# Queries and keys of a small attention layer in three TensorE blocks, and new orders on four engines, in a vision-transformer kernel

## The reference: what is computed

```python
def reference(x, ...):
    h = _L0_tok_ref(x, ...)                                   # 8 x 64 tokens x 192
    h = h + _L0_attn_ref(_layernorm(h, axis=-1), ...)
    h = h + _L0_ffn_ref(_layernorm(h, axis=-1), ...)
# attention: each token sees every 8th token of its image up to itself, itself, and the one before it
    qkv = x @ qkv_w.T + qkv_b                                  # 192 -> 3 x 192
    strided = j % stride == 0
    strided = strided & (j <= i)
    return strided | (j == i) | (j == i - 1)
# experts
    for e in range(E):                                         # 8
        w_e = jnp.sum(top_w * (top_i == e), axis=-1)[:, None]
        h = jax.nn.gelu(flat @ w1[e] + b1[e], approximate=False)   # 192 -> 768
        out = out + w_e * (h @ w2[e] + b2[e])                      # 768 -> 192
```

## Time and profile before

| | |
|---|---|
| median of 3 executions | 186.79 us (186.65 to 186.85) |
| the profiled execution | 186.15 us, of which the span (first to last instruction) is 184.4 us |
| PE busy | 172.6 us (94% of the span), 1129 matmuls |
| DVE busy | 138.7 us (75%) |
| ACT busy | 116.1 us (63%) |
| POOL busy | 84.0 us (46%) |
| DMA | 18.08 MB, mean 98 GB/s |

### The profile page before, as it was taken

How to read it: one execution, slowest core, us unless ns; L and a number is a source line. 1 busy time by engine, 2 the same in 40 slices (tenths; PEclk the granted TensorE clock), 3 DMA queues, 4 the chain that set the end, 5 groups by cost and what they waited for, 6 DMA issues and landing times.

```text
span 184.4 us, 3458 instructions
## 1 busy us (share of the span) xinstructions
PE 172.6 (94%) x1129; PEld 147.5 (80%) x1129; DVE 138.7 (75%) x311; ACT 116.1 (63%) x208; POOL 84.0 (46%) x111
## 2 busy tenths in 40 slices
PE   5898999698988989899999999999999999999994
PEld 2486589586865659789899899999999999999994
DVE  5479998678359973997787688688688688687553
ACT  2499653585416445756876875875975975973730
POOL 7876403521998216901651651661662562560000
PEclk9999999999999999999999999999999999999999
DMA  5999999100116800054005406406406400000002
GB/s 120 241 334 324 231 243 241 34 2 0 46 42 211 259 5 0 0 164 136 4 0 174 125 0 177 122 2 170 128 0 202 97 2 0 0 4 0 0 0 85
DMA packets 14979, 18.08 MB, mean 98 GB/s; under 512 B 2467, under 2 KB 10776, under 8 KB 14966
## 3 DMA queue, kind: packets, MB, share of 16 engines
q1 hardware_dynamic: 14422, 17.90, 35.5%
q10 hardware_dynamic: 544, 0.03, 0.2%
HBM read 17.14 MB, written 0.39 MB: 95 GB/s over the span
## 4 chain that ended last, share of the span: by engine, by line
PE 63%; DVE 5%; POOL 3%; issue 1%; POOLq 0%; DVEq 0%
PE ps L371 30%; PE ps L1187 18%; PE ps L1189 8%; PE ps L1237 1%; PE ps L1236 1%; PE ps L1235 1%; DVE merge L1268 1%; PE ps L383 1%; DVE big_r L1268 1%; POOL h L589 1%; POOL halo L597 1%; DVE bn L1435 1%; PE ps L378 1%; POOL halo L602 1%; POOL wsplit L330 1%
## 5 line engine op out<-in xcount | busy, mean ns | idle before, releaser
L371 PE MATMUL ps<-big_r,wsplit 128*128 128x512 f32 (+1 forms) x245 | 61.5, 387 | 0.0
L793 ACT ACTIVATE early<-ps,b1t 128x512 f32<-128x512 f32 x48 | 32.8, 683 | 29.1 <-PE ps L371 27.4
L1187 PE MATMUL ps<-wsplit,big_r 128*128 128x384 f32 x168 | 49.7, 355 | 0.7 <-DVE big_r L1268 0.7
L1268 DVE TENSOR_TENSOR big_r<-early,big_r 128x512 fp32r<-128x512 f32 x48 | 35.9, 750 | 15.8 <-ACT big_r L334 15.4
L371 PEld LDWEIGHTS ps<-big_r,wsplit 128*128 128x128 f32 x245 | 41.9, 189 | 6.3
L1189 PE MATMUL ps<-wsplit,big_r 128*128 128x192 f32 x168 | 42.1, 251 | 0.0
L1187 PEld LDWEIGHTS ps<-wsplit,big_r 128*128 128x128 f32 x168 | 31.5, 188 | 2.7 <-issue 1.1
L1189 PEld LDWEIGHTS ps<-wsplit,big_r 128*128 128x128 f32 x168 | 32.0, 190 | 1.3
L334 ACT ACTIVATE big_r<-early 128x512 fp32r<-128x512 f32 x48 | 30.4, 632 | 1.5
L1606 DVE SCALAR_TENSOR_TENSOR merge<-sq,gates,merge 128x192 f32<-128x192 f32 x32 | 26.9, 863 | 0.0
L316 POOL TENSOR_TENSOR wsplit<-stage,wsplit 128x768 fp32r<-128x768 f32 x4 | 7.4, 1848 | 19.3 <-ACT wsplit L334 15.7
(11 more groups left out here) (239 smaller groups left out, 282.0 us busy)
## 6 DMA issues: line engine op xcount, KB each, us to landing
stage<-in_L_ffn_w SPq DMA_DIRECT2D x4, 576.0 KB, 6.2
early<-in_L_ffn_w SPq DMA_DIRECT2D x4, 576.0 KB, 5.3
shifted<-in_L_tok_w SPq DMA_DIRECT2D x6, 288.0 KB, 7.0
early<-in_x SPq DMA_DIRECT2D x6, 256.0 KB, 4.8
stage<-in_L_ffn_w SPq DMA_DIRECT2D x4, 384.0 KB, 3.8
stage<-in_L_ffn_w SPq DMA_DIRECT2D x8, 192.0 KB, 4.8
early<-in_L_ffn_w SPq DMA_DIRECT2D x4, 384.0 KB, 3.1
early<-in_L_ffn_w SPq DMA_DIRECT2D x8, 192.0 KB, 4.2
```

What stands on the lines that cost most here:

```text
L371: mm = nc.tensor.matmul(dst, lhs, rhs, start=(first and n == 0), stop=(last and n == 4))
L793: nc.scalar.activation(gf[:, j % NG], ps[:, HPB[j % 4], :], ACT.Gelu, bias=b1t[:, bass.ds(k, 1)]).then_inc(s_gelu, 1)
L1187: nc.tensor.matmul(ps[:, AB[t], 0:2 * D], g_hi[:, j % NG, tok], w2c, start=(f == 0), stop=False)
L1268: return nc.vector.tensor_tensor(o, a, b, op)
```

## The change

Queries and keys together have 384 columns, three blocks of 128. The change makes them so: the first two blocks go into the two halves of bank `QB[g]`, the third into `KB[g]`. The second block then holds the last 64 columns of the queries on partitions 0 to 63 and the first 64 of the keys on partitions 64 to 127. ScalarE, which copies queries from PSUM to SBUF, moves them across partitions so that each query head stands on the partitions of its key head; three copies of 64 partitions take the place of one of 128 and one of 64. The constants (`head_of_row`, `place`, the bias columns) and the VectorE and TensorE steps that read queries and keys follow the new places.

Beside this, orders change: on ScalarE three `split_high` of expert 0 stand before `small_high(2)`, and `values(0)` before the work on `n1` of group 1; on GpSimd `near_values(0)` stands before `split_low_w2(0, 0)` and the addition to `h`; `split_low_w1(1, 1)` waits for the first `low_hidden` before its second half, and `split_low_w2(1, 1)` for the third instead of the second; on TensorE two matmuls without use (`IDLE`) stand before the transposes of `n1` of group 0, those of group 1 stand behind `strided_scores(0)`, `repeated_v(0)` before `near_by_heads(1)`, `transposed_p(1)` before `repeated_v(3)`; on VectorE `key_blocks(0)` stands before `normalised(0, 1)`, `scores(1)` before `denominators(0)`, `low_hidden(0, 0)` before `two_largest`, and the index search and two more `low_hidden` before the rest of `their_experts`.

```diff
+        HEADS_OF = (slice(4, HEADS), slice(0, 4))
+        ROWS_OF = (slice(0, P), slice(REM, P))
+        LOCAL = (slice(0, 8), slice(4, 8))
...
-        def split_low_w1(pool, e, slot):
+        def split_low_w1(pool, e, slot, ready=0):
...
             pool.wait_ge(s_w1hi, e * 2 + 2)
+            if ready:
+                pool.wait_ge(s_glo, ready)
             nc.gpsimd.tensor_tensor(ws[REM:P, W1R:W1R + F], st[REM:P, F:2 * F],
...
             split_low_w1(pool, 0, 0)
-            split_low_w2(pool, 0, 0)
-
-            pool.wait_ge(s_n, TT)
-            pool.wait_ge(s_row, 1)
-            nc.gpsimd.tensor_tensor(h[:, :, :], h[:, :, :], const_row[:, :].unsqueeze(1).broadcast_to([P, TT, D]),
-                                    ALU.add).then_inc(s_hrow, 1)
...
                 near_values(g)
+                if g == 0:
+                    split_low_w2(pool, 0, 0)
+                    pool.wait_ge(s_n, TT)
+                    pool.wait_ge(s_row, 1)
+                    nc.gpsimd.tensor_tensor(h[:, :, :], h[:, :, :],
+                                            const_row[:, :].unsqueeze(1).broadcast_to([P, TT, D]),
+                                            ALU.add).then_inc(s_hrow, 1)
...
-            split_low_w1(pool, 1, 1)
+            split_low_w1(pool, 1, 1, 1)
...
-            pool.wait_ge(s_glo, 2)
+            pool.wait_ge(s_glo, 3)
             split_low_w2(pool, 1, 1)
...
-            small_high(2)
             act.wait_ge(d_stage[0], 16 * STAGE_DMAS)
             split_high(0, 0)
             split_high(0, 1)
+            split_high(0, 2)
+            small_high(2)
...
-                nc.scalar.activation(qt[:, 0, cols], ps[:, QB[g], 0:TG], ACT.Identity,
-                                     bias=bqk[:, 0:1]).then_inc(s_qtsb, 1)
-                nc.scalar.activation(qt[0:REM, 1, cols], ps[0:REM, QB[g], TG:2 * TG], ACT.Identity,
-                                     bias=bqk[0:REM, 1:2]).then_inc(s_qtsb, 1)
+                for rows, n, of, col in ((slice(REM, P), 1, slice(0, REM), 0), (slice(0, REM), 0, slice(REM, P), 0),
+                                         (slice(REM, P), 0, slice(0, REM), 1)):
+                    nc.scalar.activation(qt[rows, n, cols], ps[of, QB[g], col * TG:(col + 1) * TG], ACT.Identity,
+                                         bias=bqk[of, col:col + 1]).then_inc(s_qtsb, 1)
...
                 triple(ps[:, QB[g], 0:TG], nx(cols), wx_(slice(0, P)), False)
-                triple(ps[0:REM, QB[g], TG:2 * TG], nx(cols), wx_(slice(P, D)), False).then_inc(s_qt, 1)
+                triple(ps[:, QB[g], TG:2 * TG], nx(cols), wx_(slice(P, 2 * P)), False).then_inc(s_qt, 1)
...
-                triple(ps[:, KB[g], 0:TG], nx(cols), wx_(slice(D, D + P)), False)
-                triple(ps[0:REM, KB[g], TG:2 * TG], nx(cols), wx_(slice(D + P, 2 * D)), False).then_inc(s_kt, 1)
+                triple(ps[:, KB[g], 0:TG], nx(cols), wx_(slice(2 * P, 3 * P)), False).then_inc(s_kt, 1)
...
             masks(1)
+            for _ in range(IDLE):
+                nc.tensor.matmul(ps[:, NTB[0], :], xh[:, 0, 0:P], xh[:, 0, :], start=True, stop=True)
             transposes(0, n1, s_n, lambda t: t + 1, NTB, s_nt, s_ndup)
...
             values(0)
-            transposes(1, n1, s_n, lambda t: t + 1, NTB, s_nt, s_ndup)
             values(1)
             pe.wait_ge(s_watraw, 1)
             masks(0)
             strided_scores(0)
+            transposes(1, n1, s_n, lambda t: t + 1, NTB, s_nt, s_ndup)
             near_by_heads(0)
...
             dve.wait_ge(s_rl, 2)
             nc.vector.tensor_copy(lgt[:], ps[0:E, RB, :]).then_inc(s_rlsb, 1)
+            low_hidden(0, 0)
             two_largest()
-            low_hidden(0, 0)
             low_hidden(0, 1)
+            experts_found()
+            low_hidden(0, 2)
             their_experts()
-            low_hidden(0, 2)
             pair(0, False, first=True)
```

74 lines of the change are left out of this document (40 added, 34 removed).

## The result

The changed kernel needs 183.42 us in the median of four runs (183.08 to 183.88), the kernel before 186.72; the ratio is 0.9824 with a 95% interval of 0.9801 to 0.9848. (186.79 was the median of before when the forecast was made, 186.72 is the one of the runs beside the change.) The profiled execution took 183.55 us, with a span of 181.8; the sum had said 183.6 and 181.85 for it.

What follows compares the result with a forecast made beforehand. TensorE's matmuls bound the kernel from 76 us, so only the first `layer2` could move: 1.86 us up to `raw` plus 0.69 us make 2.55. Median 186.79 less 2.55 gave 184.2 us, range 183.5 to 185.2.

Steps and rivals of the forecast that it cites:

- the sum: All gains ahead of the first `layer2`: 1.86 + 0.69 = 2.55 us, taken off profiled execution and median; chance 0.66.
- What bounds the kernel, and the sum's base: TensorE saturated from 76 to 168 us, so only the first `layer2` at 75.30 can move; base is the profiled execution.
- Step 1: ScalarE's order: three weight splits ahead of `small_high(2)`, so the doubling norm starts at 35.24 instead of 36.71, -1.47 us.
- the rival in small: Expert 0's weights land later than 31.84, delaying the doubling norm; 185.1 us at a landing of 33; chance 0.05.
- Step 2: Three blocks instead of four on TensorE: 0.07 us gained in group 0, nothing in group 1; ScalarE's third copy hidden.
- Step 3: Group 1's transposes behind the scores on TensorE: low part at 44.24 instead of 45.44, -1.20 us.
- Step 4: GpSimd's order: its 0.43 us wait goes, `raw` at 59.17; product into `merge` blocked by the addition until 56.56.
- Step 5: VectorE's first subtraction (`low_hidden`) ahead of the search removes TensorE's wait at the first `layer2`, -0.69 us.
- Step 6: Operand of TensorE's fourth `layer2` block, wanted at 79.80, comes in time: margin 0.1 us, no wait counted.
- more than the sum: Rival: VectorE's product before the addition, GpSimd's series less disturbed, up to 0.5 us more gain, 183.7 us; chance 0.05.
- The port: Rival: VectorE and GpSimd block each other at the shared SBUF port, 0.3 to 1.0 us less gain, 184.5-185.2; chance 0.18.
- The falling clock: Rival: TensorE's longer wait for `merge` lowers the changed kernel's clock to 1.2 GHz, up to 186.6-189 us; chance 0.06.

Runs made afterwards that it cites:

- second profiles: Kernel before and changed kernel, both unchanged, profiled and timed again: medians 186.53 and 183.28 us, profiled executions 186.62 and 183.39 us.

## Which steps of the forecast held and which failed

- **What bounds the kernel, and the sum's base:** right. The 110.9 us from the first `layer2` on did not move in any profile.
- **Step 1, 1.47 us:** right, and exact in the second profiles (2.45 us from small copy to norm became 0.98). In the medians the order brings 1.8 us alone and 2.3 by its removal; a part of the excess is the granted clock, which falls behind the idle time that this order removes, and the rest is open. The landing (32.66) was later than taken and cost 0.47 us of this step in the profiled execution, the rival in small.
- **Step 2, 0.07 us:** wrong in kind. Alone the blocks cost 0.8 to 0.9 us in the median; among the new orders they are worth nothing. The step put a price on ScalarE's third copy and none on VectorE, whose rows grew by 0.3 us a group. ScalarE's copies took 0.47 us each, as estimated, but the three fill 1.46 us where the two had filled 0.82; they stayed hidden.
- **Step 3, 1.20 us: failed in size, it should have been 1.52.** The bias product came 3.96 us behind the norm (3.93 forecast) and the transposes began 7.36 behind it (7.43 forecast). But the step let ScalarE's copy start 0.95 us behind them, as before. There the transposes took 0.91 us, since the doubling of group 1 ended only at 43.60, beside them; behind the scores it is done by 42.86, they take 0.66 in one piece, and the copy starts 0.69 behind their start. So the low part came at 8.68 instead of 9.00, and the loss of 0.27 us that the step counted did not occur.
- **Step 4:** the series took 14.05 us without a wait (14.11 forecast), and `raw` came at 59.31 (59.17): near in time from the span's start only because the late landing hid the 0.33 us of step 3. Its mechanism was partly wrong: the removed wait comes from the scores' earlier place, while GpSimd's own order gives its 0.3 us through `halo`. The blocked product into `merge` took 0.56 us and not 2: VectorE came to it only as the addition ended. TensorE's wait of 1 to 1.5 us there did not occur.
- **Step 5, 0.69 us: failed in size.** The kernel without it lost 0.87 us, and of these 0.80 hang on the gates. The term left out the 0.16 us of overlap. From `raw` to layer two the change gained 0.93 us in all.
- **Step 6:** right, the fourth block came at 79.64, just behind its subtraction (78.89 + 0.69 = 79.58).
- **The step that failed** is therefore the sum behind the norm: steps 2 to 5 were forecast at 1.08 us and brought 1.65, 0.33 more at step 3's low part (0.26 of it the copy's distance) and 0.24 more at the experts' start. With it the sum is 2.55 + 0.57 = 3.12 us and the forecast 186.79 - 3.12 = 183.7 us, inside the range. Of the 0.25 us that are left, 0.16 are the earlier input products of one pair of profiles, and 0.2 can be the clock of before (186.62 against 186.42 with the idle time filled); the runs do not part them.
- **From the profiled execution to the median:** taking the sum off the median was sound. The 0.64 us between the two were mostly the early input products of that one execution (0.45 us earlier than in the second), and they were not found again: the profiled executions of after lie 0.1 us above their medians. Left out, the forecast would have been 183.6 us, near the measured time, but only since one error covers the other; with the right sum the same step gives 186.15 - 3.12 = 183.0. For the same reason the hit on the profiled execution (183.6 against 183.55) confirmed nothing: in that pair the norm moved by 1.00 us and not by 1.47.
- **Rivals:** "more than the sum" came about, through other rows than it named. The port cost nothing on the path in this order, but 0.5 to 0.8 us where the gates or the addition stood otherwise. The falling clock was a rival of the wrong kernel: it is the kernel before that had it.

Not settled: why the clock falls in some executions and not in others of the same kernel, and how much of the differences between medians beyond the timelines' is clock.

## What to carry to other kernels

Read terms against an anchor inside the same execution (here the doubling norm), so that a late landing doesn't hide an error of another term. One profiled execution can be early or late by half a us, and so can that of the changed kernel: a forecast that hits the profiled time may do so by two errors, and the gap between a profiled execution and the median belongs in the range. When a step moves rows to a place where they no longer wait, do not carry over a distance that was measured across that wait. Before counting what a leaner engine saves, ask who feeds it: the matmuls saved here came back as waits for VectorE, and a wait can also cost the clock.

## What the runs showed of the hardware

- VectorE's products with PSUM and per-partition scalar took 0.86 to 0.87 us for two and 1.80 for four in the new layout (second halves from partition 64), and 0.73 and 1.64 us in the old one (all from partition 0). That the start partition is the cause is not shown: no run changes it alone, and in the same profiles single rows on all 128 partitions grew too, from 0.467 and 0.468 us to 0.473 and 0.484, while those on 64 went from 0.468 to 0.486 and 0.491.
- In the kernel before, which has 1.5 us of idle TensorE at 35 us, the granted clock of the whole execution was 0.991 or less in 57 of the 72 executions whose clock is on record, and with that idle time filled in none of 12. Two profiles show a fall itself, to 1.2 GHz for some 3.4 us: from 39.1 to 42.5 in the changed kernel with ScalarE's old order, and from 54.1 to 57.5, behind waits of 0.52 and 1.03 us, in the kernel with the blocks alone. 3.4 us at half clock are 0.009 of the span (an estimate), so 0.991 reads as one fall and 0.982 as two; no profile of before caught one. In the first series the executions of before with one fall and with none had the same median, 186.5 us; with two they took 187.3 or more; and in the one profile where the rest is comparable (the first of the two) a fall cost 0.9 us. The forecast's "no gap of before brought this about" held for the one profiled execution only.
- VectorE's rows with both inputs in SBUF wait for a running GpSimd row to end (1.96 us for 0.69, 1.33 for 0.56); those with an input in PSUM do not (`halo` 0.49 and `raw` 0.55 beside GpSimd). The Trainium skill ("SBUF — State Buffer", who interferes with whom) states both, and these rows agree.
